# Where a pair's small matrix products stand in TensorE's order: ahead of a group's first scores, or behind them

## The reference

```python
def proj(x, W, b, L):
    return (x @ W.T + b).reshape(B, L, NH, HD).transpose(0, 2, 1, 3)      # NH = 16 heads of HD = 16
q, k, v = proj(hs, Wq, bq, S), proj(at, Wk, bk, T), proj(at, Wv, bv, T)   # hs = layernorm(x), at = context
scores = clip(einsum('bhsd,bhtd->bhst', q, k) / 4, -50, 50), -10000 where masked, clipped again
ctx = softmax(scores) @ v
delta = layernorm(rs * (ctx @ Wo.T + bo)) * ln_gamma + ln_beta
x = x + tanh(g_xattn) * delta
# then a mixture of 8 experts: router, top 2, softmax of the two, squared relu between two products
x = x + tanh(g_ffn) * moe(layernorm(x), w_router, w_fc, w_proj)
```

## Time and profile before

| | |
|---|---|
| timed runs, median of 3 | 1163.13 us |
| profiled execution | 1154.87 us |
| its span, first to last instruction | 1152.9 us |
| mean granted TensorE clock | 0.992 of full |
| TensorE matmuls busy | 1116.1 us (97%) |
| VectorE busy | 857.2 us (74%) |
| ScalarE busy | 663.8 us (58%) |
| GpSimd busy | 156.8 us (14%) |

### The profile page before, as it was taken

The page is one execution under the profiler, slowest core; times in us unless marked ns, Lnnn a source line. Parts: engine busy times, 40 slices in busy tenths (PEclk is TensorE's granted clock), DMA queues, the critical chain, the costliest instruction groups (busy, mean ns, idle before and its releaser), DMA issues.

```text
span 1152.9 us, 55850 instructions
## 1 busy us (share of the span) xinstructions
PE 1116.1 (97%) x24824; PEld 1071.8 (93%) x24824; DVE 857.2 (74%) x1985; ACT 663.8 (58%) x845; POOL 156.8 (14%) x186
## 2 busy tenths in 40 slices
PE   6899999999999999999999999999999999999994
PEld 6899999999999999999999999999999999998994
DVE  5667777777777777777777777777777777786877
ACT  4466565656566565656556565656565665655542
POOL 0001000011111111011011111011111101022542
PEclk9899999999999999999999999999999999999997
DMA  4212221221222121222122122112122222123416
GB/s 157 65 53 70 70 70 41 77 69 56 71 77 72 60 70 52 78 63 70 58 78 71 60 72 76 54 61 79 50 77 70 68 61 77 52 73 100 132 54 172
DMA packets 44654, 84.63 MB, mean 73 GB/s; under 512 B 12866, under 2 KB 27202, under 8 KB 44418
## 3 DMA queue, kind: packets, MB, share of 16 engines
q1 hardware_dynamic: 34706, 65.62, 19.3%
q10 hardware_dynamic: 6832, 8.92, 2.4%
q0 software_dynamic: 2880, 6.53, 1.6%
HBM read 70.32 MB, written 10.79 MB: 70 GB/s over the span
## 4 chain that ended last, share of the span: by engine, by line
PE 85%; DVE 12%; issue 1%; DMA 1%; ACT 0%; POOL 0%; SPq 0%; DVEq 0%; POOLq 0%
PE v_ps L617 22%; PE k_ps L620 21%; PE sc_ps L643 19%; PE o_ps L658 11%; DVE prob L1335 3%; DVE vst L1101 2%; PE sc_ps L559 2%; DVE kl L1086 2%; PE sc_ps L561 2%; PE sc_ps L560 2%; PE k_ps L675 1%; PE k_ps L682 1%; DVE c_lo L1092 1%; DVE acc L1572 1%; DVE q_hi L1138 1%
## 5 line engine op out<-in xcount | busy, mean ns | idle before, releaser
L918 ACT ACTIVATE prob<-sc_ps,m_bias 125x896 f32<-125x896 f32 x384 | 377.1, 1008 | 325.8 <-PE sc_ps L643 325.3
L617 PE MATMUL v_ps<-wv_hi,c_hi 64*125 64x256 f32 x1520 | 311.0, 284 | 2.0 <-DVE vst L1101 1.9
L620 PE MATMUL k_ps<-c_hi,wk_hi 64*128 64x500 f32 x760 | 305.9, 403 | 0.0
L617 PE MATMUL v_ps<-wv_lo,c_hi 64*125 64x256 f32 x1520 | 301.0, 278 | 0.0
L617 PE MATMUL v_ps<-wv_hi,c_lo 64*125 64x256 f32 x1520 | 301.0, 278 | 0.0
L620 PE MATMUL k_ps<-c_lo,wk_hi 64*128 64x500 f32 x760 | 293.2, 386 | 0.0
L620 PE MATMUL k_ps<-c_hi,wk_lo 64*128 64x500 f32 x760 | 292.3, 385 | 0.0
L1101 DVE TENSOR_TENSOR vst<-v_ps,rowv 125x512 f32<-125x512 f32 x191 | 131.3, 687 | 179.4 <-PE v_ps L617 179.4
L1335 DVE TENSOR_SCALAR prob<-prob 125x896 f32<-125x896 f32 x384 | 235.3, 625 | 20.6 <-ACT prob L918 20.6
L617 PEld LDWEIGHTS v_ps<-wv_hi,c_hi 64*125 64x125 f32 x1520 | 226.0, 184 | 16.5 <-issue 8.2
L643 PE MATMUL sc_ps<-q_lo,kh 64*125 64x224 f32 x1536 | 229.8, 269 | 0.0
(11 more groups left out here) (201 smaller groups left out, 1652.4 us busy)
## 6 DMA issues: line engine op xcount, KB each, us to landing
raw<-in_ctxT SPq DMA_DIRECT2D x96, 500.0 KB, 3.5
rows<-slot_rows SPq DMA_DIRECT2D x32, 132.0 KB, 2.2
w_raw<-in_we ACTq DMA_DIRECT2D x16, 256.0 KB, 4.7
rec<-inv_scratch SPq DMA_DIRECT2D x64, 56.0 KB
expert_out<-expert_rows SPq DMA_DIRECT2D x6, 448.0 KB, 7.0
xq<-in_x ACTq DMA_DIRECT2D x16, 112.0 KB, 3.5
xr<-in_x ACTq DMA_DIRECT2D x16, 112.0 KB, 3.5
out_y<-acc SPq DMA_DIRECT2D x3, 448.0 KB, 3.1
```

The lines of the kernel that those rows point to most:

```text
L617: v_last = pe.matmul(v_ps[0:TC, j * D:(j + 1) * D], c_s[v_rows, cs], w_m[v_rows, k, :], start=begin and j == 0, stop=end, skip_group_check ...
L620: k_last = pe.matmul(k_ps[:, half, 0:TG], w[k_rows, k, ws], c_m[k_rows, :], start=begin, stop=end)
L918: act.activation(prob[0:TC, c % PB, :].rearrange("p (c n) -> p c n", c=2), sc_ps[0:TC, 2 * (c % 2):2 * (c % 2) + 2, 0:NH * S // 2], ACT.Ex ...
```

## The change

On TensorE the side work stands behind the first chunk's scores of its group, where it stood behind the four chunks' products. On ScalarE the copies of the two transposes stand behind the first exponential of the half group. On VectorE the four steps that take group 3's results out stand behind `ctx_low`; `y_low` keeps its place in the order (it moves into the branch of the even half groups, and 10 is even). No instruction is added or dropped on any engine.

```diff
@@ tensor, pair(i) @@
                             pv(*((i, c - d) if q > 0 else (i - 1, PC - d)))
-                    beside_pv(i, q, first, late, final)
                     if more:
                         kv_part(n, 0, slot, 0)
                     scores(i, c)
+                    beside_scores(i, q, first, late, final)
                     if more:
                         kv_part(n, 0, slot, 1)
@@ the function is renamed, its body is the same @@
-            def beside_pv(i, q, first, late, final):
+            def beside_scores(i, q, first, late, final):
@@ scalar, pair(i) @@
+                    if u == 11 and final:
+                        turned_high(0)
+                    exps(i, 2 * u)
                     if first and u == 2:
                         x_transposed(1)
                     if u == 10 and not late:
                         x_transposed(i + 2)
                     if u == 10 and not first:
                         y_transposed(i - 1)
-                    if u == 11 and final:
-                        turned_high(0)
-                    exps(i, 2 * u)
@@ vector, pair(i) @@
                     if not (final and q >= PG - 2):
                         ctx_low(i * PG + q + 2, half, q % 2)
-                    if u == 10 and not first:
-                        y_low(i - 1)
                     if half == 0:
+                        if u == 6:
+                            beside_scores(i, first, final)
+                        if u == 10 and not first:
+                            y_low(i - 1)
                         if more:
                             v_evac_step(i * PG + q + 1, half, (q + 1) % 2)
+            def beside_scores(i, first, final):
+                if not final:
+                    q_evac(i + 1)
+                if not first:
+                    delta(i - 1)
+                if ranked(i):
+                    slots(i)
+                if router_pair(i, 3) is not None:
+                    logits_evac(router_pair(i, 3), logit_ps[0])
@@ vector, before_clips, u == 6 @@
                     o_evac_step(i, 0)
...
```

More of the change, by code:

```diff
@@ L1392, in before_clips @@
                     o_evac_step(i, 0)
[L1393 to L1400, removed]
                 if u == 2 and final:
```

## The result

The changed kernel takes 1171.76 us (median of 6 runs, 1170.20 to 1171.95), the kernel before 1162.82 beside it (1161.54 to 1163.44): ratio 1.0075, 95% interval 1.0062 to 1.0088. The forecast was 1163.1 with a range up to 1166.8, and it is wrong: the change costs 9 us.

The account below looks back on a forecast made before the run. TensorE, busy 97% of the span, was taken to bound the kernel. The terms -5.5 + 5.6 + 0.2 - 0.26 gave 0.0 us on a profiled 1154.87, plus 8.26 carried along: 1163.1, range 1159.8 to 1166.8.

Parts of the forecast that it names:

- the last line of the sum: Added the 8.26 us by which timed runs exceeded the profiled 1154.87 to an unchanged execution, giving 1163.1.
- Part 1: TensorE's waits for the keys' copy and `y_row`, mainly group 5, go: 5.5 us off before the last pair.
- Part 2: Side groups pay another array turn between 64 and full rows: 0.18 us each, 5.6 us on; bounds 0 and 0.30.
- Part 3: Group 3's later VectorE steps delay the values' copy L1101: 0.02 us lost each, 0.2 us in 12 pairs.
- Part 4: Last pair: group 1 -0.42, group 3 +0.16, group 5 hidden behind a DMA; -0.26 us altogether.
- Stalls of issue: Rival: group 5's slow products (2.08 against 1.77) lose their stall under the new order, -3.6 us, 1159.4; chance 0.05.
- The turns are free: Rival: waits go and array turns cost nothing, -6 us or half that, 1157 to 1160.3; chance 0.11.
- groups 0, 1, 2 or 4 change by more than 0.05: Sign of a wrong forecast: groups without side work were to stay at 10.06 us.
- The wait is only moved: Rival: the keys' copy holds the first scores instead, so nothing goes and 5.6 us comes, 1168.7; chance 0.05.
- VectorE's queue becomes the wait: Rival: group 3's kv part waits for L1101 behind slipped steps, 1166 to 1169 with dearer turns; chance 0.17.

Follow-up runs that it names:

- before_again: The kernel before, unchanged, profiled once more: 1155.51 us, beside timed runs of 1154.38.
- before_third: The kernel before, unchanged, profiled in a later comparison: 1161.29 us, where its timed runs take 1162.23.
- after_third: The changed kernel, unchanged, run again: 1170.90 us beside 1162.23 for the kernel before, ratio 1.0073.
- q5_alone: Against the kernel before, only group 5's side work goes behind the first scores: 1151.61 us, ratio 0.9975.
- q5_sends_early: Against the kernel before, only group 5's side work moved, plus GpSimd's two indirect DMAs of a pair issued early: 1147.97 us, ratio 0.9940.
- q5_early_again: Same kernel as q5_sends_early, run again where the kernel before takes 1162.23: 1147.82 us, ratio 0.9871.
- run 128: Not a follow-up run; "run" is a verb here: 128 products take 1.56 us.

## Why the prediction was wrong, point by point

The step that failed is the last line of the sum: "The median of the timed runs stands 8.26 above that execution, and I carry it along". The 8.26 is no constant around the span. From the profile of before_again to that of before_third each of the pairs 3 to 12 grows by 0.69, from 64.27 to 64.96, and the two behind them by 0.3 each, 7.6 in all (pair 0 is 2 us shorter, so the spans differ by 5.8), and it lies in groups 4 and 5, the second of which the change was to shorten. Between the spans of before_third and after_third (1159.3 and 1167.5, 8.2 apart) the groups stand like this; the first column is what the forecast's parts give when they are sorted by group:

| where | forecast | measured | step |
|---|---|---|---|
| group 5, pairs 0 to 14 | -2.6 | +2.3 | Part 1: the waits were hidden |
| group 4, pairs 0 to 14 | 0 | +1.5 | not in the forecast |
| group 3, pairs 0 to 14 | +2.9 | +4.1 | Parts 2 and 3, mis-sized |
| group 1 of pair 0 | 0 | +0.3 | Part 1: no wait there |
| last pair | -0.3 | -0.6 | Part 4 |
| rest, and ahead of group 1 | 0 | +0.6 | |

**Part 1, the waits that go.** The mechanism is right on a 1154 chip, where more goes than I took (0.44 for 0.33). From before_again to q5_alone it is 0.25 between products and transposes, 0.13 and 0.06 at the two pairs of transposes. The 0.31 that the prediction took for two transposes alone was too long: they take 0.25 (528.28 to 528.53 in before_third), so it counted 0.08 where 0.14 was lost. On a 1163 chip the stall of the products had covered the wait. This is the largest miss, 4.9 of 8.2 us. "Nothing moves ahead of it, so it should stay" was said of the stall in the rival *Stalls of issue*, and it did stay; but I saw 0.3 of a stall that is 1.2 where the times were taken.

**Part 2, one more turn.** Entry into full rows as worked out. TensorE in group 3, after (two scores, the first side matmul, the next kv part), then VectorE:

```profile
511.18 0.32 PE L643 MATMUL sc_ps<-q_hi,kl 64*125 64x224 f32 x2
511.43 0.21 PE L719 MATMUL k_ps<-cum_b,ones 112*112 112x8 bf16 x1
...
513.87 0.38 PE L617 MATMUL v_ps<-wv_hi,c_hi 64*125 64x256 f32 x1
...
516.64 0.35 PE L617 MATMUL v_ps<-wv_hi,c_hi 64*125 64x256 f32 x1
```

```profile
515.80 0.69 DVE L1101 TENSOR_TENSOR vst<-v_ps,rowv 125x512 f32<-125x512 f32 x1
```

From the last scores to the side work it is 0.25 where it was 0.11: 0.14, the estimate. The Trainium skill, TensorEngine Tiling (Array Packing), section Tiling Modes, has it that a change of mode drains TensorE; the trace agrees in so far as the change costs something, 0.14 us here. The way out costs more than I took: 0.04 to 0.05 in the kv part behind and 0.04 to 0.05 in the one after that. A side group without a wait on either side pays 0.19 to 0.24 (group 3 of pairs 1 and 2, group 5 of the others) in place of 0.18, inside the bounds. *The turns are free* is out.

**Part 3, VectorE's queue.** In the rows above L1101 starts 515.80 - 513.87 = 1.93 behind the kv part, as forecast (1.94), and TensorE goes on 0.15 behind its end. The loss was to be 0.02. The wait itself is 0.01, but the kv part that starts out of it takes 1.47 where the trace has 1.37 before. Group 3 is 0.29 longer instead of 0.20 in the pairs 3 to 14 and 0.19 in pairs 1 and 2, which send and rank nothing. I cannot say whether the 0.1 is that wait; no run took it apart.

**Group 4** was costed at nothing, and "groups 0, 1, 2 or 4 change by more than 0.05" was named as the sign of a wrong forecast. It grew by 1.5 us in 12 pairs. The send of group 4 waits for a `rstd` whose input comes out of VectorE's queue (L1074). The moved steps make that queue later: L495 starts 0.66 ahead of the products before (514.42 to 515.08) and 0.50 after (519.77 to 520.27). It reaches 0.75 and 0.91 into them, and the stall is 0.24 and 0.38 (on 1163 chips). I had looked at GpSimd's sends for who waits for them, not for what they disturb.

**The rivals.** *The wait is only moved* (1168.7) and *VectorE's queue becomes the wait* (1166 to 1169) come nearest in time and are wrong in kind: no new wait of either appears, the old one was not there. In the waits view of before_third that could have been read in one row. *Stalls of issue* had the right thing and the wrong direction: it asked whether the 0.3 might vanish, and they vanish only when the sends are moved.

## What to carry to other kernels

Before a change is costed from a profile, hold the profiled execution's own time against the timed runs: 8 us of 1163 were a second way for the same program to run, and the waits of one way are hidden in the other. Where a burst of small instructions shows "issue", look at what every other engine does at that moment, GpSimd's indirect DMAs first, and move that rather than the burst; here that and the half of the change that works (group 5's) were worth 1.3% where the stalls were large. A wait is worth nothing while something else holds the same engine for longer at the same place.

## What the runs showed of the hardware

- Products of 125 x 17 by 56 run 128 in 1.56 us. With an indirect DMA of GpSimd issued beside them they took 1.87 (group 5) and 1.56 (group 4) on chips where the kernel before takes 1154, and 2.75 and 1.79 on chips where it takes 1163 (before_third, means); with the DMA elsewhere 1.56 on both (q5_sends_early, q5_early_again). On a 1163 chip the break moved with the DMA: after 71 products, after 59 in pair 13, after 16 in the last pair. Kv matmuls, which are longer, did not slow (12.52 with both DMAs beside them). What the two engines share, and what differs between the chips, stays open.
- The place of TensorE's instructions in their packets of 256: 64 instructions more at the head of the queue made the kernels 4.6% and 6.0% slower, and the waits print 21.3 and 36.2 us of stalls, up to 1.3 and 1.7 each, in the first scores behind the products. The 10 or 5 filling instructions of a pair are worth 0.8% in the kernel before.
- Entering full rows behind a stream of 64 rows costs 0.14 us of TensorE (0.25 for 0.11), and going back 0.04 to 0.05 in each of the two kv parts behind.
